# Two up tiles multiplied by halves of the tokens, and one-hot tables with the tokens innermost

## The reference, cut to what matters

```python
x = x + attention(layernorm(x), ctx_1024, mask, Wq, bq, Wk, bk, Wv, bv, Wo, bo)   # 16 heads of 32
xf = layernorm(x).reshape(4096, 512)
route_prob = softmax(xf @ Ws + bs, axis=-1).T             # 8 experts x 4096 tokens
route_vals, routes = top_k(route_prob, 512)               # per expert
xin = xf[routes]
h = gelu(einsum('ekd,edf->ekf', xin, W1) + b1[:, None])   # F = 2048
out = (einsum('ekf,efd->ekd', h, W2) + b2[:, None]) * route_vals[..., None]
x = x + zeros(4096, 512).at[routes.reshape(-1)].add(out.reshape(-1, 512))
```

## Time and profile before

| | us |
|---|---|
| median of 3 runs | 1670.79 |
| lowest, highest run | 1665.35, 1675.45 |
| profiled execution | 1667.8 |
| its span | 1666.0 |
| PE busy in the span | 1597.9 (96%) |
| DVE busy | 1113.7 (67%) |
| ACT busy | 976.8 (59%) |
| POOL busy | 300.0 (18%) |

### The profile page before, as it was taken

The page is one execution under the profiler, slowest core; times in us unless marked ns, Lnnn a source line. Parts: engine busy times, 40 slices in busy tenths (PEclk is TensorE's granted clock), DMA queues, the critical chain, the costliest instruction groups (busy, mean ns, idle before and its releaser), DMA issues.

```text
span 1666.0 us, 22367 instructions
## 1 busy us (share of the span) xinstructions
PE 1597.9 (96%) x7847; PEld 1162.0 (70%) x7847; DVE 1113.7 (67%) x1950; ACT 976.8 (59%) x2115; POOL 300.0 (18%) x396
## 2 busy tenths in 40 slices
PE   7999999999999999999886999999999999999997
PEld 5556666666666666666544787888888888888885
DVE  7676878878788797787746577765554555454543
ACT  5788898989989899798872223222222223232331
POOL 6220221302213022130300201002020202020110
PEclk9999999999999999999997999999999999999999
DMA  5643654626547364462611423416252524343330
GB/s 179 184 123 95 193 145 140 208 80 205 144 132 207 87 200 147 134 192 83 190 67 64 127 89 90 152 57 184 76 159 101 159 91 144 101 132 119 102 110 26
DMA packets 131271, 217.27 MB, mean 130 GB/s; under 512 B 17116, under 2 KB 51056, under 8 KB 131160
## 3 DMA queue, kind: packets, MB, share of 16 engines
q1 hardware_dynamic: 114520, 173.23, 33.1%
q0 software_dynamic: 16640, 42.61, 9.6%
HBM read 157.45 MB, written 57.82 MB: 129 GB/s over the span
## 4 chain that ended last, share of the span: by engine, by line
PE 86%; DVE 7%; ACT 2%; DMA 2%; issue 2%; POOL 0%; SPq 0%; DVEq 0%; POOLq 0%; ACTq 0%
PE ps_gen L888 9%; PE ps_gen L890 9%; PE ps_gen L889 9%; PE ps_gen L1905 7%; PE ps_gen L2069 7%; PE ps_gen L2071 7%; PE ps_gen L2070 7%; PE ps_gen L1873 7%; PE ps_att L1916 7%; PE ps_gen L1855 3%; PE ps_gen L1856 3%; PE ps_gen L1857 3%; PE ps_gen L1932 2%; PE ps_gen L1933 2%; PE ps_gen L1934 2%
## 5 line engine op out<-in xcount | busy, mean ns | idle before, releaser
L1476 DVE TENSOR_REDUCE nmax<-ps_gen 128x1 f32<-128x512 f32 x512 | 331.9, 684 | 79.5 <-PE ps_gen L1873 77.8
L1292 ACT ACTIVATE p_ring<-ps_gen,keep_scale 128x512 f32<-128x512 f32 x512 | 341.3, 702 | 44.2 <-PE ps_gen L1905 30.7
L1280 ACT ACTIVATE ps_gen<-ps_gen,nmax 128x512 f32<-128x512 f32 x512 | 342.6, 676 | 33.6 <-DVE nmax L1476 33.4
L1349 ACT ACTIVATE gel<-ps_gen,b_cols 128x512 f32<-128x512 f32 x128 | 88.3, 690 | 448.8 <-PE ps_gen L890 448.7
L1737 DVE TENSOR_TENSOR gel_lo<-gel,gel_hi 128x512 fp32r<-128x512 f32 x126 | 87.3, 692 | 281.6 <-ACT gel_hi L1350 277.3
L888 PE MATMUL ps_gen<-hT_hi,w_hi 128*128 128x512 f32 x512 | 202.2, 395 | 0.2 <-DVE hT_lo L1730 0.2
L1873 PE MATMUL ps_gen<-kst,qst 97*128 97x512 f32 x512 | 193.0, 424 | 8.6 <-issue 4.6
L890 PE MATMUL ps_gen<-hT_hi,w_lo 128*128 128x512 f32 x512 | 199.5, 390 | 0.0
L889 PE MATMUL ps_gen<-hT_lo,w_hi 128*128 128x512 f32 x512 | 199.4, 389 | 0.0
L1905 PE MATMUL ps_gen<-qst,kst 99*128 99x512 f32 x512 | 194.9, 424 | 3.8 <-DMA qst<-by_row 3.1
L2069 PE MATMUL ps_gen<-w_hi,gel_hi 128*128 128x512 f32 x504 | 198.1, 393 | 0.0
(11 more groups left out here) (218 smaller groups left out, 2672.0 us busy)
## 6 DMA issues: line engine op xcount, KB each, us to landing
w_raw<-in_L_ffn_W SPq DMA_DIRECT2D x128, 512.0 KB, 3.3
kst<-qk_rows SPq DMA_DIRECT2D x93, 256.0 KB, 4.0
qst<-qk_rows SPq DMA_DIRECT2D x93, 256.0 KB, 4.1
x_in<-in_x POOLq DMA_DIRECT2D x60, 256.0 KB, 4.1
out_x<-x_in SPq DMA_DIRECT2D x32, 256.0 KB, 3.3
qk_rows<-kT_hi SPq DMA_DIRECT2D x31, 256.0 KB, 2.3
qk_rows<-kT_lo SPq DMA_DIRECT2D x31, 256.0 KB, 3.7
qk_rows<-qT_hi SPq DMA_DIRECT2D x31, 256.0 KB, 2.0
```

What stands on the lines that cost most here:

```text
L1280: e.activation(psum[:, :], psum[:, :], ACT.Exp, bias=nmax[g % 2][:, c], scale=-1.0, accum_out=den[g % 2][:, c]).then_inc(drained_sem("max" ...
L1292: e.activation(p_ring[n % NP_][:, :], ps("score", g, kt, h)[:, :], ACT.Exp, scale=keep_scale[:, b:b + 1]).then_inc(drained_sem("score", g, ...
L1476: e.tensor_reduce(nmax[g % 2][:, h * TB + t:h * TB + t + 1], ps("max", g, h, t)[:, :], AX.X, ALU.min).then_inc(s_min, 1)
```

## The change

The up tiles 0 and 1 of expert 0 are each done as two halves of 256 tokens (`up_half`): for each half 4 high x high matmuls, 4 high x low, 4 low x high, so 24 matmuls of 256 columns for each tile. The high x high part of the first half of tile 0 stands between turns 2 and 3, in place of two `keep_busy` matmuls; the rest of both first halves follows turn 3, in place of the last six, and then the second halves of tile 0 and of tile 1. up(2) now stands ahead of down(0). On DVE `rows_lo(0, 1)` is moved ahead of `early_w1_lo(0)`, and `early_w2_lo(0)` behind `rows_lo(0, 3)`.

The one-hot tables are ordered expert, digit, block, so that the 32 blocks lie side by side; `dig_a` and `dig_b` hold each digit 32 times, and the operands of one block in `list_slots` have a step of 32 elements (64 bytes) between columns.

```diff
@@ -649,8 +649,8 @@
         tri = sb(p3, "tri", [P, P], BF16)
         after = sb(p3, "after", [P, P], BF16)
         tok = sb(p3, "tok", [P, NT], F16)
-        dig_a = sb(p3, "dig_a", [P, A_N], F16)
-        dig_b = sb(p3, "dig_b", [P, B_N], F16)
+        dig_a = sb(p3, "dig_a", [P, A_N, NT], F16)
+        dig_b = sb(p3, "dig_b", [P, B_N, NT], F16)
         count_of = sb(p3, "count_of", [P, 8], I32)
         shift_of = {g: sb(p3, f"shift_of{len(g)}", [P, len(SHIFTS[g])], I32) for g in (FIRST, REST)}
         sb(p3, "pad4", [P, 96])
@@ -1150,8 +1150,8 @@
                         made(e.iota(shift_of[group][:, :], pattern=[[-BITS[group], len(SHIFTS[group])]], base=SHIFTS[group][0],
                                     channel_multiplier=0))
                     made(e.iota(tok[:, :], pattern=[[P, NT]], base=-TOK0, channel_multiplier=1, allow_small_or_imprecise_dtypes=True))
-                    made(e.iota(dig_a[:, :], pattern=[[1, A_N]], base=0, channel_multiplier=0, allow_small_or_imprecise_dtypes=True))
-                    made(e.iota(dig_b[:, :], pattern=[[1, B_N]], base=0, channel_multiplier=0, allow_small_or_imprecise_dtypes=True))
+                    made(e.iota(dig_a[:, :, :], pattern=[[1, A_N], [0, NT]], base=0, channel_multiplier=0, allow_small_or_imprecise_dtypes=True))
+                    made(e.iota(dig_b[:, :, :], pattern=[[1, B_N], [0, NT]], base=0, channel_multiplier=0, allow_small_or_imprecise_dtypes=True))
                     made(e.memset(ones_h[:, :], 1.0))
                     made(e.affine_select(out=tri[:, :], in_=ones_h[:, :], compare_op=ALU.is_ge, fill=0.0,
                                          base=0, pattern=[[1, P]], channel_multiplier=-1))
@@ -1657,27 +1657,30 @@
                 e.tensor_copy(high_h[:, c, :], high_i[:, c, :]).then_inc(*mark())
 
             def hot_view(tile, ne, width):
-                return tile[:, 0:NT * ne * width].rearrange("p (t e a) -> p t e a", e=ne, a=width)
+                return tile[:, 0:NT * ne * width].rearrange("p (e a t) -> p e a t", e=ne, a=width)
+
+            def digit_of(digits, exps, width):
+                return (digits[:, exps[0]:exps[0] + len(exps), :].rearrange("p e (a t) -> p e a t", a=1)
+                        .to_broadcast([P, len(exps), width, NT]))
+
+            def digits_all(table, ne, width):
+                return table[:, :, :].rearrange("p (e a) t -> p e a t", e=1).to_broadcast([P, ne, width, NT])
 
             def hot_low(exps):
-                ne, e0 = len(exps), exps[0]
+                ne = len(exps)
                 on.wait_ge(s_listed, listed_before(exps))
                 on.wait_ge(s_sel, n_sel)
-                e.tensor_tensor(hot_view(hot_a, ne, A_N),
-                                low_h[:, e0:e0 + ne, :].rearrange("p e (t a) -> p t e a", a=1).to_broadcast([P, NT, ne, A_N]),
-                                dig_a[:, :].rearrange("p (t e a) -> p t e a", t=1, e=1).to_broadcast([P, NT, ne, A_N]),
+                e.tensor_tensor(hot_view(hot_a, ne, A_N), digit_of(low_h, exps, A_N), digits_all(dig_a, ne, A_N),
                                 ALU.is_equal).then_inc(*mark())
 
             def hot_high(exps):
-                ne, e0 = len(exps), exps[0]
+                ne = len(exps)
                 on.wait_ge(s_listed, listed_before(exps))
-                e.tensor_tensor(hot_view(hot_b, ne, B_N),
-                                high_h[:, e0:e0 + ne, :].rearrange("p e (t a) -> p t e a", a=1).to_broadcast([P, NT, ne, B_N]),
-                                dig_b[:, :].rearrange("p (t e a) -> p t e a", t=1, e=1).to_broadcast([P, NT, ne, B_N]),
+                e.tensor_tensor(hot_view(hot_b, ne, B_N), digit_of(high_h, exps, B_N), digits_all(dig_b, ne, B_N),
                                 ALU.is_equal).then_inc(*mark())
                 on.wait_ge(s_sel, n_sel)
                 e.tensor_tensor(hot_view(hot_b, ne, B_N), hot_view(hot_b, ne, B_N),
-                                tok[:, :].rearrange("p (t e a) -> p t e a", e=1, a=1).to_broadcast([P, NT, ne, B_N]),
+                                tok[:, :].rearrange("p (e a t) -> p e a t", e=1, a=1).to_broadcast([P, ne, B_N, NT]),
                                 ALU.mult).then_inc(s_hot, 1)
 
             def write_idx(exps):
@@ -1760,11 +1763,11 @@
                 e.tensor_tensor(w2s[n][1][:, :, :], w2_raw[n][:, :, :], raw(w2s[n][0][:, :, :]), ALU.subtract).then_inc(s_split_early, 1)
 
             rows_lo(0, 0)
+            rows_lo(0, 1)
             early_w1_lo(0)
-            rows_lo(0, 1)
-            early_w2_lo(0)
             rows_lo(0, 2)
             rows_lo(0, 3)
+            early_w2_lo(0)
             early_w1_lo(1)
             early_w2_lo(1)
             gelu_lo(0)
@@ -1999,8 +2002,8 @@
 
             def list_slots(exps):
                 ne = len(exps)
-                a = hot_a[:, 0:NT * ne * A_N].rearrange("p (t m) -> p t m", t=NT)
-                b = hot_b[:, 0:NT * ne * B_N].rearrange("p (t m) -> p t m", t=NT)
+                a = hot_a[:, 0:NT * ne * A_N].rearrange("p (m t) -> p t m", t=NT)
+                b = hot_b[:, 0:NT * ne * B_N].rearrange("p (m t) -> p t m", t=NT)
                 on.wait_ge(s_hot, listed_before(exps) + 1)
                 if exps == (1,):
                     on.wait_ge(s_hT_lo, TT)
@@ -2078,12 +2081,42 @@
                         last.then_inc(s_y_full, 1)
                 last.then_inc(s_down, 1)
 
-            for tt in range(TT):
+            def up_half(m, n2, high):
+                w = w1s[0]
+                col = slice(m * P, (m + 1) * P)
+                toks = slice(n2 * (K // 2), (n2 + 1) * (K // 2))
+                psum = ps_up[m][:, toks]
+                if high:
+                    on.wait_ge(s_hT_hi, 2 * n2 + 2)
+                    on.wait_ge(s_split_act, 1)
+                    for c in range(DC):
+                        e.matmul(psum, lhsT=w[0][:, c, col], rhs=hT[0][0][:, c, toks], start=(c == 0), stop=False)
+                    return
+                on.wait_ge(s_hT_lo, 2 * n2 + 2)
+                for c in range(DC):
+                    e.matmul(psum, lhsT=w[0][:, c, col], rhs=hT[0][1][:, c, toks], start=False, stop=False)
+                on.wait_ge(*w1_split(0))
+                for c in range(DC):
+                    last = e.matmul(psum, lhsT=w[1][:, c, col], rhs=hT[0][0][:, c, toks], start=False, stop=(c == DC - 1))
+                if n2 == 1:
+                    last.then_inc(s_up, 1)
+
+            for tt in range(3):
                 turn_rows(0, tt)
-                keep_busy(2 if tt < TT - 1 else 6, ps_up[1])
-            up(0)
+                if tt < 2:
+                    keep_busy(2, ps_up[1])
+            up_half(0, 0, True)
+            turn_rows(0, 3)
+            up_half(1, 0, True)
+            up_half(0, 0, False)
+            up_half(1, 0, False)
+            for m in range(2):
+                up_half(m, 1, True)
+                up_half(m, 1, False)
+            up(2)
             for i, (ex, j) in enumerate(order[:BODY]):
-                up(i + 1)
+                if i > 1:
+                    up(i + 1)
                 route_beside(i)
                 down(i)
                 if ex + 1 < E and NF - 6 <= j < NF - 2:
```

## The result

The changed kernel is slower: 1696.08 us, median of 6 runs (1692.17 to 1698.00), against 1667.50 of 6 runs of the kernel before. The ratio is 1.0159 with a 95% interval of 1.0146 to 1.0171, so 28.6 us more. The forecast was 1672.3, in a range from 1665 to 1680. The profiled execution took 1692.17 us, its span 1690.4.

A forecast was written before the change was run, and what follows sets the result against it. PE was taken as the bound, a full queue of matmuls behind about 931 us. Halves -1.8, tables -1.1 and lists +4.4 gave +1.5 on 1667.8, so 1669.3, or 1672.3 on the median's scale; range 1665 to 1680.

The forecast's parts named there:

- The halves: Expert 0's first up tiles on PE: half matmuls fill the time between turns in place of keep_busy, gaining 1.8 us.
- The pace of 0.12 us: Half matmuls of 256 columns on PE would start 0.12 us apart, between 0.108 and 0.188.
- the wait of 0.2 us on gelu(0): On PE, up(2), now next after the halves, would wait for gelu(0), costing 0.2 us.
- SP's load of piece 3: Weight load queued behind DVE's low parts: some 2.3 us later than 930.31, hidden because first used at 958.41.
- The tables on DVE: Expert 0's one-hot writes on DVE would go at two elements per cycle, gaining 1.1 us.
- The lists on PE: 160 small matmuls in five lists would slow by DVE's step factor of 1.85, losing 4.4 us.
- DVE's absolute price on the loaded columns: Rival for the five lists: PE pays 1.94 ns per loaded column, +10.7 us, so 1678.6; chance 0.16.
- The clock: Rival: PE's clock falls; PE has as much work between the turns as before, so only a share of the tail.
- Filling the digit tables: POOL writes 1536 elements instead of 48, covered by its idle time: cost nothing, up to 3 us if uncovered.
- The whole stage after 940 us changes its pace: Listed sign that the prediction is wrong, about the expert stage after 940 us; no size given.

The follow-up runs named there:

- e4: The kernel before with only the new order of tiles 0 and 1 on PE and DVE, old tables and addresses: 1667.47 us, ratio 0.9992.
- f1: The kernel after with pad4 larger by 1120 bytes, so hT and all behind lie 4096 bytes beyond their place before: 1678.99 us, ratio 1.0076.
- e1: The kernel before with unused tile pad4 larger by 2976 bytes, moving hT, gel and the rest as the larger tables do: 1687.60 us, ratio 1.0106.

## Why the prediction was wrong

Two things failed: a term that stood at nothing without a price, the place of the tiles behind the larger digit tables (17 to 19 us), and the cost of the lists on PE, put at 4.4 us and measured at 9.7, with 3.9 us of lower clock on top that the forecast left out. By its own steps, in their order:

**The halves** were predicted at -1.8 us and gave -1.56 (e4). The pace of 0.12 us came out exactly, and so did the wait of 0.2 us on gelu(0). Nothing moved behind them was missed: SP's load of piece 3 went out at 927.83, 3.15 us behind turn 3 (924.68) where it was 0.84 behind it in the earlier trace rows, so 2.3 us later as worked out, and the time from tile 3 on is that of before in e4.

**The tables on DVE**: -1.1 predicted, -1.04 measured. From 512 to 1024 elements a write grows by 0.27 us, 0.53 ns an element, where it grew by 1.07 ns (0.68 to 1.23 us). The rule of the page "VectorE: DVE Perf Modes" of the Trainium skill (What auto-detection actually checks), that this needs all tensors 16-bit with step 1, holds here: 1024 elements in 0.69 us where the old order, with one source repeated innermost, took 1.23.

**The lists on PE** were mis-sized: 4.4 us predicted, 9.7 measured (4.0 - 1.9 and 11.2 - 3.6 in the groups above). The matmul grew from 0.028 to 0.060 us with 32 loaded columns and from 0.035 to 0.115 with 64, that is 1.8 to 1.9 ns a loaded column. This is the rival "DVE's absolute price on the loaded columns", which gave 62 and 124 ns from the earlier trace rows. I had taken the ratio of that row in place of its price, since the price was another engine's; the price was what carried over. A ratio on top of the old pace would have been right only if that pace had been reading alone. The rule of the page "Advanced Engine Details and Errata" (Memory Cachelines) of the Trainium skill, 16 bytes with at least two hits each, agrees with the steps tried on the loaded operand: 4 bytes free, 16 and 64 paid. The streamed operand, at 64 bytes, showed no price; whether its reading is hidden under the longer load was not tried.

**The clock** was given no more than a share of the tail. It fell to 0.50 at two of the three lists of pairs in the kernel after. The tiles around the three lists took 6.78, 7.27 and 6.78 us before and 11.99, 11.42 and 9.44 after: 12.0 us more, of which 7.6 are the lists themselves and some 0.5 the pace, so 3.9 for the clock. In f1 they took 9.34, 11.26 and 9.34: 9.1 more, 1.4 of it the clock, which fell once. That its median lies 3 us above this execution may be more such falls, since its other three executions had a lower mean clock (0.983, 0.984 and 0.982 against 0.985); there is no trace of them.

**Filling the digit tables** was costed at nothing, and this is the step whose failure cost most. The filling itself was indeed hidden. POOL's timeline after:

```profile
817.71 1.14 POOL L1153 IOTA dig_a<- 128x1024 f16 x1
818.92 0.62 POOL L1154 IOTA dig_b<- 128x512 f16 x1
...
827.37 1.03 POOL L1174 DMA_DIRECT2D qst<-by_row  x2 [5.48 <-DVE by_row L1484]
```

It still sat idle for 5.48 us ahead of its next task, against 6.96 in the earlier trace rows. But the same two lines of the diff that make the tables larger move every tile allocated behind them, and I had looked at them only as work for POOL. "The whole stage after 940 us changes its pace" stood among what would make the prediction wrong; its cause stood nowhere, and it had no price.

The account of the 28.9 us that the kernel after takes more, from `hot_a` to the last gelu: tables and first list -0.0; from the gather to tile 3 -0.5 (halves -1.6, expert 1's list +0.95, and a rest of 0.1, which is no more than the slower pace does here: f1, with the old distance, took 0.26 less over this stretch); from tile 3 on +29.4, of which 12.0 around the lists and 17.4 in the other 121 tiles, 0.144 us each. The padding alone (e1) cost 17.8 from tile 3 on, 0.143 a tile. The two agree, so no large term is missing. With the distance restored, f1's 9.1 us from tile 3 on are the three tiles with lists and nothing else, and its median of 1678.99 is about where the rival on the loaded columns had put the whole change (1678.6). That is in part luck: the rival had the lists 1.0 us too dear and left the clock out, and its scale stood 3 us too high. The prediction put the median 3.0 us above the profiled execution of before, from three runs (1670.79); with six runs it is 1667.5, at that execution. Taken as differences, the rival says +7.8 us, and f1's medians say +11.4 (1678.99 against 1667.64), its profile +8.3 from `hot_a` to the last gelu.

So without the move the change would have stayed just inside the range of 1665 to 1680, but not for the reasons of the forecast: in f1 the lists cost 9.7 us and the clock 1.4 more where the forecast had 4.4 for both.

## What to carry to other kernels

A table that grows moves every tile allocated behind it, and that is a part of the change: print the addresses before and after, and if the pace of untouched matmuls has changed, put unused bytes in front to separate the move from the rest. When data are turned round to please the engine that writes them, keep what lies innermost as short as that engine needs (two elements here), so that the engine that reads them, and loads weights from them, keeps neighbours. For an access whose price is only known from another engine, the absolute price is as good a guess as the ratio; where they differ by more than a factor of two in the sum, as 4.4 and 10.7 us did here, the range has to reach both.

## What the runs showed of the hardware

- A matmul of 512 fp32r columns with its load took 0.2267 us when the place of the loaded and of the streamed tile differed by a multiple of 256 bytes in a partition (moves of 0, 256, 3072 and 4096 bytes, and of both tiles together by 32), 0.233 to 0.234 when it differed by 128 or 160 beyond one, and 0.232 at 192. Whether a move of both tiles together by 128 is free, whether other sizes and types see it, and what causes it, was not tried.
- A matmul with a load of 32 or 64 f16 columns that lie 16 or 64 bytes apart took 1.8 to 2.0 ns for each loaded column; with 4 bytes between them it is as quick as with neighbours (0.028 and 0.035 us).
- PE was busy without a gap in the profile through 3.65 us of small matmuls with such loads, and yet the granted clock went to its lower level, 1.2 GHz, at 12 of the 15 lists of 3.6 to 4.0 us in the five profiles that have them, in the list or right behind it; at lists of 1.12 us it did not. PE went through the list itself in the same 3.65 us whether the clock fell in it or not.
